# Who makes the low halves of the expert weights: VectorE alone behind the seventh chunk, where GpSimd made nine of them

## What is computed

```python
x = x + tanh(g_xattn) * xattn(layernorm(x), ctx, mask, W, b)
x = x + tanh(g_ffn)   * ffn(layernorm(x), w_router, fc1_w, fc2_w, gate_w, up_w, down_w)
...
# ffn: 2048 tokens of width 256, 8 experts, the 2 best per token
top_logits, top_idx = top_k(h @ w_router, 2)
scores = softmax(top_logits)
# per token and chosen expert e: (silu(h @ fc1_w[e][:, :256]) * (h @ fc1_w[e][:, 256:])) @ fc2_w[e]
# and for every token the shared part: (silu(h @ gate_w) * (h @ up_w)) @ down_w
```

## Time and profile before

| | before |
|---|---|
| median of three runs | 239.54 us (239.11 to 240.22) |
| the profiled execution: its time, and its span from the first to the last instruction | 239.18 us, 237.4 us |
| TensorE (PE) busy | 221.6 us, 93% of the span |
| VectorE (DVE) busy | 173.8 us, 73% |
| ScalarE (ACT) busy | 130.0 us, 55% |
| GpSimd (POOL) busy | 125.4 us, 53% |

### The profile page before, as it was taken

How to read it: one execution, slowest core, us unless ns; L and a number is a source line. 1 busy time by engine, 2 the same in 40 slices (tenths; PEclk the granted TensorE clock), 3 DMA queues, 4 the chain that set the end, 5 groups by cost and what they waited for, 6 DMA issues and landing times.

```text
span 237.4 us, 5269 instructions
## 1 busy us (share of the span) xinstructions
PE 221.6 (93%) x1417; PEld 193.4 (81%) x1417; DVE 173.8 (73%) x514; ACT 130.0 (55%) x316; POOL 125.4 (53%) x177
## 2 busy tenths in 40 slices
PE   7988999999899999999599999999999999999980
PEld 7778899978688888888488888888888888887860
DVE  1978797797668899999967656656656656655895
ACT  2556888772647644555126556556556556555320
POOL 1698997564777877887601344344344343343600
PEclk9999999999999999999999999999999999999998
DMA  4899940000122215322242533433433432109777
GB/s 157 269 394 404 405 184 0 0 3 22 45 94 77 80 70 203 133 71 93 76 127 67 145 105 91 120 105 93 115 103 89 123 90 68 49 29 305 260 233 303
DMA packets 18131, 32.05 MB, mean 135 GB/s; under 512 B 3046, under 2 KB 9323, under 8 KB 18104
## 3 DMA queue, kind: packets, MB, share of 16 engines
q1 hardware_dynamic: 14096, 22.28, 29.6%
q0 software_dynamic: 3408, 8.46, 9.6%
q10 hardware_dynamic: 600, 0.97, 1.1%
HBM read 19.95 MB, written 12.67 MB: 137 GB/s over the span
## 4 chain that ended last, share of the span: by engine, by line
PE 45%; POOL 8%; issue 6%; DVE 3%; DMA 2%; ACT 0%; SPq 0%; DVEq 0%; POOLq 0%
PE bank L987 38%; POOL rows L388 6%; PE bank L1232 4%; PE bank L1252 4%; POOL ew_lo L243 2%; DVE acc L959 1%; DMA rows<-hrows,slot 1%; DMA hrows<-rows 1%; DVE act_lo L630 1%; DVE acc L702 1%; SPq L280 0%; DVE act L922 0%; ACT act_hi L443 0%; ACT act L581 0%; DVEq L62 0%
## 5 line engine op out<-in xcount | busy, mean ns | idle before, releaser
L430 POOL DMA_INDIRECT parts<-y_out,dst x39 | 38.8, 995 | 69.7 <-DVE dst L916 66.0
L922 DVE TENSOR_TENSOR act<-act,bank 128x256 f32<-128x256 f32 x39 | 16.4, 421 | 34.4 <-ACT act L581 32.6
L388 POOL DMA_INDIRECT rows<-hrows,slot x32 | 35.1, 1097 | 12.3 <-issue 12.1
L581 ACT ACTIVATE act<-bank 128x256 f32<-128x256 f32 x39 | 15.0, 384 | 37.5 <-PE bank L987 37.5
L987 PE MATMUL bank<-ew_hi,m_xt_hi 128*128 x78 | 30.9, 396 | 0.1
L987 PE MATMUL bank<-ew_hi,m_xt_lo 128*128 x78 | 30.8, 395 | 0.0
L987 PE MATMUL bank<-ew_lo,m_xt_hi 128*128 x78 | 30.7, 394 | 0.0
L987 PE MATMUL bank<-ew_hi,act_hi 128*128 x78 | 25.2, 323 | 0.2 <-DVE act_lo L630 0.2
L443 ACT ACTIVATE act_hi<-act 128x512 fp32r<-128x512 f32 x16 | 10.1, 631 | 21.8 <-DVE act L689 21.8
L987 PE MATMUL bank<-ew_hi,act_lo 128*128 x78 | 21.9, 281 | 0.0
L987 PE MATMUL bank<-ew_lo,act_hi 128*128 x78 | 21.9, 281 | 0.0
(11 more groups left out here) (182 smaller groups left out, 656.8 us busy)
## 6 DMA issues: line engine op xcount, KB each, us to landing
ew_raw<-in_chunks SPq DMA_DIRECT2D x12, 512.0 KB, 10.7
hrows<-rows SPq DMA_DIRECT2D x39, 130.0 KB, 2.3
low_buf<-parts SPq DMA_DIRECT2D x4, 512.0 KB, 4.2
high_buf<-parts SPq DMA_DIRECT2D x4, 512.0 KB, 5.1
acc<-in_x SPq DMA_DIRECT2D x7, 256.0 KB, 5.7
sw_raw<-in_chunks SPq DMA_DIRECT2D x3, 512.0 KB, 8.4
out<-acc SPq DMA_DIRECT2D x3, 512.0 KB, 3.4
rows<-pad_rows SPq DMA_DIRECT2D x9, 130.0 KB, 2.5
```

The source lines that it names most:

```text
L388: pool.indirect_dma_start(out=rows, out_offset=bass.IndirectOffsetOnAxis(ap=slot[:, h, k, i:i + 1], axis=0), in_=hrows[:, HT * h + i, :], ...
L430: pool.indirect_dma_start(out=parts, out_offset=bass.IndirectOffsetOnAxis(ap=dst[:, t:t + 1], axis=0), in_=y_out[:, t % SLOTS, :], in_offs ...
L581: a.activation(act[:, p, 0:I], M_H[p][:, 0:I], ACT.Silu).then_inc(s["m_sil"], 1)
L922: TT(act[:, p, 0:I], act[:, p, 0:I], M_H[p][:, I:2 * I], ALU.mult).then_inc(s["m_prod"], 1)
```

## The change

GpSimd keeps chunks 0 to 6 and makes no other low half: its eight later ones go, and its scatters follow each other. VectorE makes all 23 behind the seventh: `LATER` now gives it one in unit 0, three in unit 2, one in unit 3, two in unit 4, one each in units 5, 6 and 7, three in unit 8, one in unit 9, and three each in units 10, 11 and 12. ScalarE makes the high halves of chunks 7 to 10 ahead of `norm_second(NG - 2)`, and then two a unit instead of three in units 3 to 5; its wait for the attention's last product (`mt_ps`) moves from chunk 7 to chunk 12 (`FREE`).

```diff
-MID = tuple(IN_A + 2 * i for i in range(5))
-LAST = tuple(range(CHUNKS - 3, CHUNKS))
-LATER = {3: 1, 4: 1, 5: 1, 6: 1, 7: 1, 8: 1, 9: 2, 10: 2, 11: 2, 12: 3}
+FREE = SCH + 6
+LATER = {0: 1, 1: 0, 2: 3, 3: 1, 4: 2, 5: 1, 6: 1, 7: 1, 8: 3, 9: 1, 10: 3, 11: 3, 12: 3}
...
         def by_pool(i):
-            return i < IN_A or i in MID + LAST
+            return i < IN_A
...
-            scatter(0, 3, 8)
-            cut_lo(pool, MID[0])
-            scatter(0, 8, 12)
-            cut_lo(pool, MID[1])
-            scatter(0, 12, 2 * HT)
-            cut_lo(pool, MID[2])
+            scatter(0, 3, 2 * HT)
             weight_fields(1)
-            scatter(1, 0, 6)
-            cut_lo(pool, MID[3])
-            scatter(1, 6, 11)
-            cut_lo(pool, MID[4])
-            scatter(1, 11, 2 * HT)
-            for i in LAST:
-                cut_lo(pool, i)
+            scatter(1, 0, 2 * HT)
...
-                if i == IN_A:
+                if i == FREE:
                     after(a, "mt_ps", NG)
...
             turn_h(NG - 3)
+            for i in range(IN_A, IN_A + 4):
+                cut_hi(i)
 
             norm_second(NG - 2)
...
-            i = IN_A
+            i = IN_A + 4
...
-                more = 3 if n < 6 else 2
+                more = 2 if n < U0 - 2 else 1
...
             stats_second(NG - 1)
+            cut_later(0)
             product_lo(0)
...
             turn_h(NG - 1)
+            cut_later(2)
             product_lo(2)
```

More of the change, by code:

```diff
@@ L783, in cut_later @@
             def cut_later(u):
-                mine = [i for i in range(IN_A, CHUNKS) if i not in MID + LAST]
+                mine = range(IN_A, CHUNKS)
                 first = sum(m for w, m in LATER.items() if w < u)
@@ L787, in cut_later @@
                     cut_lo(v, i)
-                    after(v, "chunk_lv", mine.index(i) + 1)
+                    after(v, "chunk_lv", i - IN_A + 1)
             turn_x(1)
@@ L1268, in _ @@
             m_turn_x(1, 1)
-            after(pe, "chunk_lp", IN_A + len(MID + LAST))
-            after(pe, "chunk_lv", CHUNKS - IN_A - len(MID + LAST))
+            after(pe, "chunk_lp", IN_A)
+            after(pe, "chunk_lv", CHUNKS - IN_A)
             after(pe, "sil", U0)
```

## The result

| | before | after |
|---|---|---|
| median | 239.87 us (239.11 to 240.22, 4 runs) | 250.08 us (249.02 to 251.13, 4 runs) |
| the profiled execution: time, span | 239.18, 237.4 us | 251.13, 249.4 us |

What follows compares the result with a forecast made beforehand. TensorE bounds the tile stage, GpSimd's scatters and low halves the chain ahead of it. Gains of 2.58, 0.22 and 0.1 less 0.1 make 2.8 us: 239.54 becomes 236.7, range 236.0 to 237.3, 75%.

Steps and rivals of the forecast that it cites:

- GpSimd's side: Scatters up to the first tile: without low halves the last starts near 105, the tile is ready at 111 instead of 117.24.
- the 4 us of cover: At the first tile: it would be ready some 4 us ahead of TensorE, hiding any dearer scatters.
- upstream TensorE is full: Ahead of the first tile: TensorE is busy 12.00 of 12 us between 100 and 112.
- The last scatter near 105: Sign on GpSimd: the last scatter, at 111.40 before, should start near 105.
- Low halves near 686 ns, none over 1 us: Sign on VectorE: all 23 low halves should take near 686 ns, unblocked by GpSimd, none above 1 us.
- third rival: Units 8 to 12: VectorE becomes the bound; at 1.66 us a low half, 4.6 us slower, 244.1; 4%.
- break-even: Units 8 to 12: a low half costing 1.27 us on VectorE eats the 2.8 us gain; beyond it the kernel is slower.
- second rival: At the first tile: `act_lo` or a late tile replaces the wait, gain 0.3 or less, 239.2 to 239.5; 8%.
- first rival: Ahead of the tiles: a new wait at `pick`, early path or ScalarE leaves gain 1.2 to 2.3, 237.2 to 238.3; 13%.
- early path: GpSimd's two scatters ahead of `rstd_second(7)`: a VectorE low half beside them costs 0 to 0.52, taken as 0.1 us.
- The 2.58 at the tile: TensorE starts the down product of unit 12 at 115.35 instead of 117.93, a gain of 2.58 us.
- The sum as a whole: Whole kernel: 2.58 at the tile, 0.22 ahead of unit 10, 0.1 transpose overlap, less 0.1: 2.8 us; profiled execution 236.4.

Runs made afterwards that it cites:

- e2: Kernel before, with GpSimd's five low halves among the scatters moved behind the last scatter, so the scatters run unbroken: 257.72 us, ratio 1.0689.
- e1: Changed kernel with GpSimd waiting 1.72 us (three writes of zeros) at each of the five places among the scatters where a low half stood: 245.73 us, ratio 1.0199.
- e10: Changed kernel with a write of 128 by 256 zeros on GpSimd behind every scatter, awaited only behind the next: 238.24 us, ratio 0.9915.
- e8: Changed kernel with a write of 128 by 128 zeros on GpSimd behind every scatter: median 242.67 us, two runs at 238.37 and 239.55, two near 245.8.
- e12: Changed kernel with one write of zeros (0.55 us) awaited on GpSimd at three places among the scatters: 238.71 us, ratio 0.9932.
- e13: Changed kernel with zeros written behind each scatter, 128 by 256 in the first half, 128 by 128 in the second, testing a fitted backlog: 239.35 us, ratio 0.9972.
- e7: Changed kernel with three pauses of 1.72 us among the first half's scatters alone; the second half's sixteen follow each other: 239.56 us, ratio 0.9992.
- e15: e12 with eight tiny ScalarE instructions more in each of units 3 to 12, each signalling a counter of its own: 238.75 us, ratio 0.994.
- e16: e12 with the same eighty tiny ScalarE instructions, without the signals: 238.52 us, ratio 0.9942.
- e9: e2 with pauses of 1.72 us among the first half's scatters alone: 248.23 us, ratio 1.0316.
- e11: Changed kernel's scatters with three low halves left on GpSimd, VectorE making twenty: two runs at 239.35 and 239.76, two at 246.19 and 247.39 us.
- e5: Changed kernel with one write of zeros (0.55 us) awaited on GpSimd at each of five places among the scatters: 238.89 us, ratio 0.9942.

## Why the prediction was wrong

The step that failed is the one on GpSimd's side: that a scatter's price was unknown "in one point", between 967 and 1487 ns for GpSimd, and that I "count nothing for it, because the 4 us of cover hide it". The price of a scatter isn't only GpSimd's time. Packed to 1.33 us apart, the scatters cost TensorE 2.85 us in units 4 and 5, 8.23 in unit 9 and 1.50 of slow clock in unit 10: 12.6 us that no rival of mine held. I had asked what each moved instruction does to its own engine and its port neighbour, VectorE, and not what their bunching does to the rest. The same omission stands in "upstream TensorE is full": true of before, and taken for granted of after. That the run alone is enough for the slow stretches is shown (e2), and so is that spreading it out with nothing else changed takes them away (e1, e10).

- **The last scatter near 105**: 107.27, in a trace that was 1.88 late at unit 4 and in which the second half's first scatter waited 2.88 for its slots, behind the first slow stretch. Without the two it would have been near 102.5, earlier than I had taken, as the scatters didn't get longer.
- **Low halves near 686 ns, none over 1 us**: 687 on the mean. Right, in after and in e10.
- **VectorE keeps up** (third rival, 4%): it does. In e10 it waits 0.72 for TensorE in units 11 and 12, and none of its low halves took over 0.76 us, where the break-even was 1.27.
- **Late scatters or `act_lo` in place of the wait** (second rival): not in after, where both are in time. In e10 the tile is late by 1.84, since the spread delays the scatters: the second half's sixteen take 24.9 us from the first start to the last, where after's take 20.0.
- **New waits in front** (first rival): no hole at `pick`; ScalarE's four high halves don't delay group 7, which e8 turns 0.17 us later than before and e12, with the same early part, 0.15 earlier (65.39); 0.1 was in the sum for the early path.
- **The 2.58 at the tile**: 2.82 measured up to the experts' first product, where the sum has 2.68 with the overlap.
- **The sum as a whole** held for a kernel without the trouble: e10's profiled execution took 238.21 us and TensorE waited 1.84 of it for the tile, which leaves 236.4, my number for the profiled execution. That the 1.84 would come off in full is argued, not shown; e13, meant to show it, ran into late signals again.

What stays open is what scatters and TensorE share. Transfer time is unlikely: the DMA engines were busy for 0.36 of the stretch, and for the same 0.36 in e7 between 90 and 112, where TensorE was busy throughout. Late loading of instructions is unlikely too: between 98 and 110 the instruction queues moved one packet in after, and three in e10, which has no late signal. It isn't the number of instructions or signals as such, as far as the time of the two runs with ScalarE's eighty tells (e15, e16). The Trainium skill (NOTIFIC — the notification-queue block, 7.1 Overflow: three behaviours, one of which stalls the engine) says that the block which writes the engines' records to memory holds its producers back when its internal pipeline is full. No run here shows whether that is at work. Every execution here is listed with its span and clock, so each wrote such records, and it also stays open how a run without them would come out. Scatters of fewer rows, which would part the number of transfers from their bytes, weren't tried, since half of each scatter would leave rows of the table unwritten that the tiles read. Whether the debt of one run is carried into the next is open as well; e7 and e9 fit both that and the pace. And the fitted backlog fell with e13, so of the border no more is known than that it lies near 1.5 us here, for scatters of 128 rows of 1,040 bytes.

## What to carry to other kernels

Work that stands between indirect transfers on GpSimd may be what keeps them apart; before it is taken away, look at how close together they will come, and count on a price for the engines that have nothing to do with them. Where an instruction starts long after its releaser's work ended, or waits without a named releaser while another engine idles on "issue", signals may come late, as they did here: look then for what runs densely at that time, not at the instruction that waits. And when a moved piece frees an engine, try it once with something idle in the old place, which tells the gain of the move from the loss of the gap.

## What the runs showed of the hardware

- Indirect transfers of 128 rows by 1,040 bytes, issued 1.28 to 1.34 us apart for ten or more in a row, slowed TensorE to one instruction in 0.70 or 1.40 us, delayed its signals by up to 11.97 us (`product(7)` of e2, at 109.53), and stretched eight issues of SyncE from 8.95 to 15.00 us (18.09 in e2; 8.69 to 11.81 in the other runs). At 1.38 to 1.49 only the signals were late, by up to 5.6 us (e9). VectorE's own signals were nearly in time: `product(8)` of after ends at 110.98 and ScalarE goes on at 111.02; the latest, in e13, took 0.98. The scatters took their 0.98 us all the while, with VectorE standing still; beside its work they took up to 1.47 (after, at 89.92).
- It ends within 2 to 3 us of the last scatter (108.25 to 110.29 in after, 107.33 to 109.53 in e2).
- Near the border the same program gave two kinds of time, 6 to 8 us apart, in e8 and e11.
- Eight low halves back to back on GpSimd (9.85 us) hold one of VectorE's for 7.84 us (e9, from 114.28), where it takes 0.69 alone: VectorE's two-input instruction, begun 2.56 us into the eight, ended 0.55 behind the last of them.
- Between two scatters that are 0.30 us apart, a write of zeros that isn't awaited there adds less than its own time (0.22 us makes 0.39, 0.33 makes 0.49; e8, e10), and one that is awaited adds more (0.55 us makes 1.34; e5).
